# Two moves in an attention kernel on one core: P1 copies ahead of T4's split, and one pass for the norms

## The reference

```python
q = einsum('bnd,ed->bne', x, Wq); k = einsum('bnd,ed->bne', x, Wk); v = einsum('bnd,ed->bne', x, Wv)
rel = einsum('bnd,bmd->bnm', q, k)
rel = adjacency.T[None, :, :] * rel
rel = rel / norm(rel, axis=2, keepdims=True)
y = x + einsum('bnm,bmd->bnd', rel, v)
out = (y - mean(y)) / sqrt(var(y) + 1e-5)      # over the last axis
```

## Time and profile before

| | |
|---|---|
| median of 3 runs | 2206.69 us |
| profiled execution | 2207.88 us |
| its span, first to last instruction | 2206.1 us |
| mean granted TensorE clock | 0.957 |
| TensorE matmul busy | 2057.3 us (93%), 8688 instructions |
| VectorE busy | 1531.9 us (69%) |
| ScalarE busy | 702.6 us (32%) |
| GpSimd busy | 934.1 us (42%) |
| DMA | 265.45 MB, mean 120 GB/s |

### The profile page before, as it was taken

The page is one execution under the profiler, slowest core; times in us unless marked ns, Lnnn a source line. Parts: engine busy times, 40 slices in busy tenths (PEclk is TensorE's granted clock), DMA queues, the critical chain, the costliest instruction groups (busy, mean ns, idle before and its releaser), DMA issues.

```text
span 2206.1 us, 26336 instructions
## 1 busy us (share of the span) xinstructions
PE 2057.3 (93%) x8688; PEld 1680.3 (76%) x8688; DVE 1531.9 (69%) x2487; ACT 702.6 (32%) x1016; POOL 934.1 (42%) x645
## 2 busy tenths in 40 slices
PE   5999999999999999999999999999999999999998
PEld 4777787777877777877777877778777787777786
DVE  6676676766767677676767667677676776767664
ACT  4332323333232332323323233232333323233230
POOL 2633426344353443435434363342634435344341
PEclk8999999999999999999999999999999999999999
DMA  6333333333423234232333323333323342333401
GB/s 238 124 129 119 143 114 114 109 120 137 137 86 128 109 128 147 84 131 99 140 135 124 130 77 136 122 143 114 114 109 119 137 146 77 124 114 132 144 19 57
DMA packets 70444, 265.45 MB, mean 120 GB/s; under 512 B 7328, under 2 KB 7328, under 8 KB 66208
## 3 DMA queue, kind: packets, MB, share of 16 engines
q1 hardware_dynamic: 70432, 265.32, 33.0%
HBM read 225.97 MB, written 39.32 MB: 120 GB/s over the span
## 4 chain that ended last, share of the span: by engine, by line
PE 77%; DVE 11%; POOL 6%; issue 3%; ACT 1%; DMA 0%; SPq 0%; DVEq 0%; POOLq 0%; ACTq 0%
PE bank L339 26%; PE bank L340 26%; PE bank L341 26%; DVE quad_sums L715 4%; POOL yv L806 2%; POOL rel L802 2%; POOL rel L797 2%; DVE yv L615 1%; DVE squares L708 1%; DVE block_sums L710 1%; DVE rel L636 1%; DVE yv L696 1%; ACT yv L490 0%; DVE rel L643 0%; ACT yv L545 0%
## 5 line engine op out<-in xcount | busy, mean ns | idle before, releaser
L339 PE MATMUL bank<-yv 128*128 128x512 f32 x1024 | 415.1, 405 | 62.7 <-DVE yv L696 62.7
L339 PE MATMUL bank<-yv,x_hi 128*128 128x512 f32 x896 | 367.0, 410 | 53.3 <-ACT rel L520 51.6
L340 PE MATMUL bank<-yv 128*128 128x512 f32 x1024 | 413.4, 404 | 0.0
L341 PE MATMUL bank<-yv 128*128 128x512 f32 x1024 | 411.9, 402 | 0.0
L829 POOL TENSOR_TENSOR square_sum<-square_sum,squares 128x512 f32<-128x512 f32 x224 | 319.2, 1425 | 171.2 <-ACT squares L532 160.7
L340 PE MATMUL bank<-yv,x_hi 128*128 128x512 f32 x896 | 361.7, 404 | 0.0
L341 PE MATMUL bank<-yv,x_lo 128*128 128x512 f32 x896 | 360.6, 402 | 0.0
L847 POOL TENSOR_TENSOR rstd<-var_eps,minus_half 128x1 f32<-128x1 f32 x128 | 144.5, 1129 | 406.6 <-DVE var_eps L732 406.6
L339 PEld LDWEIGHTS bank<-yv 128*128 128x128 f32 x1024 | 201.2, 197 | 112.4 <-DVE yv L696 69.5
L339 PEld LDWEIGHTS bank<-yv,x_hi 128*128 128x128 f32 x896 | 176.6, 197 | 103.2 <-ACT rel L520 58.4
L541 ACT ACTIVATE yv<-rel 128x1024 fp32r<-128x1024 f32 x128 | 135.5, 1058 | 362.2 <-PE bank L341 362.2
(11 more groups left out here) (75 smaller groups left out, 3150.8 us busy)
## 6 DMA issues: line engine op xcount, KB each, us to landing
scr<-adj SPq DMA_DIRECT2D x128, 512.0 KB, 5.4
aw<-a_kept SPq DMA_DIRECT2D x15, 3584.0 KB, 11.2
scr<-xT SPq DMA_DIRECT2D x32, 1024.0 KB, 6.8
res<-x SPq DMA_DIRECT2D x128, 256.0 KB, 2.7
aw<-w_kept SPq DMA_DIRECT2D x16, 2048.0 KB, 7.8
out<-res SPq DMA_DIRECT2D x128, 256.0 KB, 2.0
a_kept<-aw SPq DMA_DIRECT2D x1, 3584.0 KB, 16.6
w_kept<-yv SPq DMA_DIRECT2D x1, 2048.0 KB, 6.3
```

Source lines behind the costliest of these rows:

```text
L339: pe.matmul(bank_ap, l_hi, r_hi, start=first and i == 0, stop=False, skip_group_check=on)
L340: pe.matmul(bank_ap, l_hi, r_lo, start=False, stop=False, skip_group_check=on)
L341: mm = pe.matmul(bank_ap, l_lo, r_hi, start=False, stop=i == len(pairs) - 1, skip_group_check=on)
```

## The change

On ScalarE the two copies of P1 of the first pair stand ahead of the two high parts of T4 instead of behind them. On VectorE one `norms` takes both halves: two transposes, one sum over both, 16 copies of 32 x 8 in place of twice 16 of 32 x 4, one last sum. It stands behind v tile 3. The third chunk (t = 2) moves behind v tile 7, on ScalarE and VectorE. GpSimd raises all eight columns to -1/2 in one instruction.

```diff
@@ ScalarE
                     y_hi_piece(b, B21, j, y_b21_raw[j])
+
+            def y_last_block(b):
                 for j in range(2):
                     act.wait_ge(y_t4, b * 2 + (j + 1))
                     y_hi_piece(b, T4, j, y_t4_raw[j])
...
                 y_blocks(b)
                 s_copy(b, 0)
                 s_copy(b, 1)
+                y_last_block(b)
                 for name, i in square_order[0:6]:
                     square(b, name, i)
...
                 for m in range(MT):
                     v_piece(b, m)
-                    if 1 <= m <= CRING:
+                    if m in (1, 2):
                         chunk(b, m - 1)
+                chunk(b, 2)
@@ VectorE
-            def norms(b, h):
-                n = b * HALVES + h
+            def norms(b):
                 dve.wait_ge(square_added, b * ADDED + (ADDED + SQRING))
-                blocks_t = squares[:, h, :]
-                dve.transpose(blocks_t, square_sum[:, h, :]).then_inc(blocks_turned, 1)
-                dve.wait_ge(blocks_turned, n + HALVES + 1)
-                dve.tensor_reduce(block_sums[:, :], blocks_t.rearrange("p (c q) -> p c q", q=Q),
+                for h in range(HALVES):
+                    dve.transpose(squares[:, h, :], square_sum[:, h, :]).then_inc(blocks_turned, 1)
+                dve.wait_ge(blocks_turned, b * HALVES + (HALVES + HALVES))
+                dve.tensor_reduce(block_sums[:, :], squares[:, :, :].rearrange("p h (c q) -> p (h c) q", q=Q),
                                   AX.X, ALU.add).then_inc(blocks_summed, 1)
-                dve.wait_ge(blocks_summed, n + 1)
+                dve.wait_ge(blocks_summed, b + 1)
                 for to in range(P // Q):
                     for of in range(P // Q):
                         dve.tensor_copy(quad_sums[Q * to:Q * (to + 1), :, of],
                                         block_sums[Q * of:Q * (of + 1), to::P // Q]).then_inc(quads_placed, 1)
-                dve.wait_ge(quads_placed, b * (HALVES * COPIES) + (h + 1) * COPIES)
-                dve.tensor_reduce(norm2[:, HT * h:HT * (h + 1)], quad_sums[:, :, :], AX.X, ALU.add).then_inc(norm2_made, 1)
+                dve.wait_ge(quads_placed, b * COPIES + COPIES)
+                dve.tensor_reduce(norm2[:, :], quad_sums[:, :, :], AX.X, ALU.add).then_inc(norm2_made, 1)
...
                 for m in range(MT):
                     v_piece(b, m)
-                    if 1 <= m <= CRING:
+                    if m in (1, 2):
                         chunk(b, m - 1)
-                    if m in (4, 5):
-                        norms(b, m - 4)
+                    if m == 3:
+                        norms(b)
+                chunk(b, 2)
@@ GpSimd
-                power_norm(b, 0)
-                power_norm(b, 1)
+                power_norm(b)
```

More of the change, by code:

```diff
@@ L69, in adjacency_attention_layernorm @@
         res = sb("res", [P, RRING, D], F32)
-        block_sums = sb("block_sums", [P, BANK // Q], F32)
-        quad_sums = sb("quad_sums", [P, HT, P // Q], F32)
+        block_sums = sb("block_sums", [P, N // Q], F32)
+        quad_sums = sb("quad_sums", [P, MT, P // Q], F32)
         norm2 = sb("norm2", [P, MT], F32)
         rnorm = sb("rnorm", [P, MT], F32)
-        minus_half = sb("minus_half", [P, HT], F32)
+        minus_half = sb("minus_half", [P, MT], F32)
         stats = sb("stats", [P, 6], F32)
@@ L722, in output @@
                 dve.wait_ge(res_loaded[slot], b * (2 * DMA) + (t // RRING + 1) * DMA)
-                dve.wait_ge(rnorm_made, b * HALVES + (t // HT + 1))
+                dve.wait_ge(rnorm_made, b + 1)
                 dve.wait_ge(o_done, b * MT + (t + 1))
@@ L838, in s_blocks, with power_norm @@
                         add_square(b, name, i)
[L840 to L843, removed]
+            def power_norm(b):
+                pool.wait_ge(norm2_made, b + 1)
+                pool.tensor_tensor(rnorm[:, :], norm2[:, :], minus_half[:, :], ALU.pow).then_inc(rnorm_made, 1)
             def power_var(b, t):
```

## The result

The changed kernel takes 2035.54 us, the median of 4 runs (2034.88 to 2035.99), against 2206.48 us for the kernel before in the same comparison: a ratio of 0.9224, with an interval from 0.9208 to 0.924. Its profiled execution took 2035.14 us, for a span of 2033.0 us. The forecast was 2033 us.

What follows compares the result with a forecast made beforehand. The prediction took TensorE's matmul stream plus two pauses per batch and their half-clock stretches as the bound. Scores 35.5, outputs 65.3 and clock 74, less 1, gave 174 us off: 2033 us (2026 to 2042, chance 0.64).

Steps and rivals of the forecast that it cites:

- What bounds the kernel: TensorE's matmul stream plus interruptions: PE waits 51.6 us for copies of P1 and 62.7 us for a v tile.
- Copies of P1: Scores: copying P1 ahead of T4's split cuts the gap from 3.39 to 1.17 us, worth 35.5 us.
- The norm pass: Outputs: one joint pass of 5.8 us behind v tile 3 removes the whole 4.08 us gap, worth 65.3 us.
- Chunk 2: Moved behind v tile 7, its low part is done by 1074.2 and needed at 1081.9.
- rival B: VectorE limits the outputs, 2059 us, or the joint pass takes its upper bound, 2057 us; chance 0.17 for both.
- The clock: TensorE stays at 2.4 GHz through the whole loop: 74 us, 36 in the scores and 38 at the outputs.
- Rival A: The clock still falls in the scores: +36 us, 2069 us; chance 0.09.
- Rivals C and D: C: P1 edit fails, scores gap stays, 2105 us, chance 0.05. D: joint pass so long the kernel is slower, 0.02.
- The sum: 35.5 + 65.3 + 74, less 1 for rests, gives 174: 2034 us profiled, 2033 us median.

Runs made afterwards that it cites:

- the first edit alone: The kernel before with only the copies of P1 moved ahead of T4's split on ScalarE: 2128.41 us, ratio 0.9642.
- the second: The kernel after with T4's split again ahead of the copies of P1, the joint norm pass kept behind v tile 3: 2078.17 us, ratio 0.9414.
- the one with no pause at all: The kernel after with B22's two low parts on VectorE moved behind the first two block sums of the scores' first pair: 2008.31 us, ratio 0.9101.

## Why the prediction was right, point by point

**What bounds the kernel.** Right. Two waits of PE were named; with one gone and the other cut to a third, and with the half-clock stretches behind both gone, the span fell by 173.1 us.

**Copies of P1.** Right in size and cause. The pause was to be 1.17 us and is 1.19 to 1.23, and the low part of B21 ends it. GpSimd's share in that, which the prediction took from a comparison of two rows and the Trainium skill ("SBUF — State Buffer", "Who interferes with whom"), is shown by the kernel in which GpSimd waits: 0.69 us in place of 1.7. One of the two rows was misread, though: GpSimd is not idle beside the 1.29 us pair at 1074.39,

```profile
1074.42 1.01 POOL L842 TENSOR_TENSOR rnorm<-norm,minus_half 128x4 f32<-128x4 f32 x1 [4.24 <-DVE norm L718]
```

and that pair reads PSUM for one input, so it could not show by itself what slows a pair with both inputs in SBUF. That closing the pause would be worth 19 us was 2 us short (2035.5 - 2014.3 = 21), since every short pause also costs 0.10 us at the restart.

**The norm pass.** Right: 5.8 us were worked out and 5.8 measured. The choice between a fixed cost per copy and a cost by size, which had 3 us between its ends, went to the fixed cost: 0.05 us more for 16 copies of twice the size. The move and the merger were priced together. The runs part them: with two passes in that place 1.8 us of pause remain, 32 us in all.

**Chunk 2.** Its move costs nothing, as said. That it also brings nothing was not said; the run shows it.

**The outputs behind it (rival B).** The chain of VectorE was worked out in advance to leave 1.8 us of cover for chunk 5. In the profile after, PE needs it at 1114.70 + 27.2 = 1141.9, and DVE ends it at 1138.45 + 1.22 = 1139.67:

```profile
1126.81 2.35 DVE L582 TENSOR_TENSOR x_lo<-scr,x_hi 128x1024 fp32r<-128x1024 f32 x2
...
1136.62 0.74 DVE L728 SCALAR_TENSOR_TENSOR res<-bank,rnorm,res 128x512 f32<-128x512 f32 x1
...
1138.45 1.22 DVE L705 TENSOR_TENSOR yv<-rel,yv 128x1024 fp32r<-128x1024 f32 x1
```

2.2 us of cover are left, and no row of PE waits for line 705. From X11's low part to the output of tile 2 it is 9.81 us, as it was 9.83 in the earlier trace rows.

**The clock.** The term of 74 us is right in total and wrong as a sum by place. I take the time between two starts of PE beyond 0.2267 us wherever the two are more than 0.24 and at most 0.6 us apart, behind the loading: 79 us in the trace of before, 7 after, which are 72 us. With 35 us from the scores pauses, 65 from the outputs and 1.7 from a shorter wait at the start this makes 174, where the span fell by 173.1 us. But "36 of it in the scores and 38 at the outputs" supposed that a pause carries its stretch with it. The same measure gives 34 us for the first edit alone, where 79 - 36 = 43 should have been left, and 16 for the second, where it should have been 79 - 38 = 41. The forecast came out because the change took away every pause behind which the clock falls, so nothing hung on which ones did. For one edit alone the step was wrong by 7 and by 25 us of time.

**Rival A.** It didn't come: none of the 96 pauses of 1.2 us, 16 in each of the six kernels that have them, has a stretch behind it, and none of the 16 of 1.8 us. But the argument against it was weaker than it looked. That the clock outlasts 3.1 idle us in one row doesn't make shorter pauses safe: pauses of 2.6 us had a stretch in 5 of 16 cases. The pause left here is a little under half of that and not a third of the shortest that is followed by a fall. The runs have no pause between 1.8 and 2.6 us, so how near 1.8 us is to a fall stays open.

**Rivals C and D.** Neither came. The copies of P1 start at 1057.60, behind the third of the parts before T4 and ahead of T4's, which begins at 1058.56. The 16 wider copies take 3.13 us, 0.20 each.

**The sum.** It is 2.5 us short, and little of this is in the terms. The span was to fall by 174 us and fell by 173.1: the scores pauses gave 0.7 less than worked out and the clock 2 less, since the restarts behind the short pauses stay, while 1 us had been set aside for rests and the wait at the start was 1.7 us shorter. This last is chance: between the kernels of this study that wait goes from 19.1 to 21.3 us. The larger part is the step from the profiled execution to the median: the one before lay 1.2 us above its median, and the forecast carried that over; the one after lies 0.4 us below its own.

## What to carry to other kernels

Before moving an instruction off the end of a wait, list every other condition of the waiting instruction and when each is met: the next one sets the size of the gain, and here the pause that is left was foreseen to 0.06 us. Where a step is late because another engine's instructions slow it, a later start for that other engine or an earlier one for the step can close what the fix leaves (21 and 27 us here). Don't price the clock pause by pause: when some long pauses go, the stretches behind those that stay change too (34 us were left in place of 43, and 16 in place of 41).

## What the runs showed of the hardware that was not expected

- Whether TensorE's clock falls to 1.2 GHz behind a pause is not settled by the pause's length alone. Pauses of 1.2 us: 0 of 96. 1.8 us: 0 of 16. 2.6 us: 5 of 16, every third batch. 3.4 us: 16 of 16 in the kernel before, 5 of 16 and then 2 of 16 in two executions of one kernel. 4.1 us: 16 of 16 in two kernels. What is common is an order in time (every third, alternately long and short, neighbours in groups) that differs between kernels and, in the one kernel profiled twice, between executions. The fall can come as late as 1.5 us after PE has started again. A stretch costs 1.5 to 2.9 us, the restart included. What in the chip sets the order was not tried.
- The time of one program varies with it: with 5 stretches in the scores the kernel with the norm pass alone took 2079.80 us, with 2 it took 2075.11. Over its first four runs the kernel with the norm pass alone ran in 2075.06 to 2079.8 us, 4.7 us apart, the one with no pause at all in 2007.9 to 2008.93, 1.0 us apart.
- Small copies on VectorE of 32 x 4 and of 32 x 8 elements take nearly the same time (3.08 and 3.13 us for 16).
- An instruction of VectorE with two inputs in SBUF and GpSimd's sums delay each other: 1.7 us in place of 0.69 for the one, 1.71 in place of 1.29 for the other.
